# Finishing each target tile of graph attention inside its edge loop, with the turned tiles in the dead rows of the queries

## What is computed

```python
hn = _batch_norm(h, bn1_g, bn1_b)
Q, K, V = (hn @ Wq), (hn @ Wk), (hn @ Wv)          # by heads of 16
score = clip(sum(K[src] * Q[dst]) / 4, -5, 5)
a = exp(score - smax[dst]); a = a / segment_sum(a, dst)[dst]
wV = segment_sum(V[src] * a, dst)
h2 = h + wV @ Wo + bo
h3 = _batch_norm(h2, bn2_g, bn2_b)                 # statistics over all nodes
return h2 + relu(h3 @ W1 + b1) @ W2 + b2
...
aggregated = segment_sum(x[src], tgt)              # the last layer
out = relu((x + aggregated / counts) @ W.T + b)
```

## Time and profile before

| | before |
|---|---|
| median of 3 runs | 1333.84 us (1333.36 to 1334.45) |
| the profiled execution's own time | 1335.18 us |
| its span | 1333.2 us |
| instructions | 18242 |
| PE busy | 990.6 us (74%) |
| DVE busy | 867.2 us (65%) |
| ACT busy | 523.6 us (39%) |
| POOL busy | 413.0 us (31%) |
| mean granted clock of PE | 0.833 |

### The profile page before, as it was taken

How to read it: one execution, slowest core, us unless ns; L and a number is a source line. 1 busy time by engine, 2 the same in 40 slices (tenths; PEclk the granted TensorE clock), 3 DMA queues, 4 the chain that set the end, 5 groups by cost and what they waited for, 6 DMA issues and landing times. The chain is left out here.

```text
span 1333.2 us, 18242 instructions
## 1 busy us (share of the span) xinstructions
PE 990.6 (74%) x6074; PEld 622.3 (47%) x6074; DVE 867.2 (65%) x2126; ACT 523.6 (39%) x1007; POOL 413.0 (31%) x516
## 2 busy tenths in 40 slices
PE   1289989999999998894655565656656565557997
PEld 1168845645556454454433343434434333345554
DVE  4879946734434467466377877777877777764343
ACT  1289913111111111112456555556655556424210
POOL 4000000000000000001277777777777777720000
PEclk9999999999999999896865766666666766568999
DMA  6000061000000000000543333333333333319000
GB/s 156 26 1 1 1 211 34 1 9 0 9 1 0 17 16 23 12 1 24 154 123 104 106 106 104 106 105 106 107 105 106 107 105 105 107 44 226 12 24 26
DMA packets 49496, 87.78 MB, mean 66 GB/s; under 512 B 12384, under 2 KB 35315, under 8 KB 49161
## 3 DMA queue, kind: packets, MB, share of 16 engines
q0 software_dynamic: 20608, 55.20, 14.4%
q1 hardware_dynamic: 26312, 29.89, 8.3%
q10 hardware_dynamic: 2492, 1.61, 0.5%
HBM read 70.68 MB, written 15.98 MB: 65 GB/s over the span
## 5 line engine op out<-in xcount | busy, mean ns | idle before, releaser
L1413 POOL DMA_INDIRECT counts_all<-kv_d,counts_all x416 | 394.4, 948 | 154.7 <-issue 145.9
L867 PE MATMUL bank<-counts_all,parts 125*128 (+2 forms) x1750 | 344.4, 355 | 19.5 <-DVE parts L1047 9.7
L867 PEld LDWEIGHTS bank<-counts_all,parts 125*128 125x128 f16 x1750 | 159.8, 98 | 190.9 <-DVE parts L1047 11.0
L1553 PE MATMUL bank<-counts_all 125*128 125x128 f16 x1230 | 133.9, 288 | 83.3 <-ACT counts_all L1619 82.9
L1299 POOL IOTA iota_n<- 128x256 f16 x1 | 0.3, 349 | 562.1 <-POOLq L854 562.1
L1553 PEld LDWEIGHTS bank<-counts_all 125*128 125x128 f16 x1230 | 110.1, 133 | 126.6 <-ACT counts_all L1619 126.3
L1542 PE MATMUL bank<-rel_rows,ident_h 104*128 104x512 f16 x104 | 56.9, 547 | 124.6 <-ACT away L1609 123.9
L1483 DVE TENSOR_TENSOR counts_all<-counts_all,bank 128x512 f32<-128x512 f32 x104 | 71.5, 687 | 117.6 <-DMA counts_all<-kv_d,counts_all 117.6
L1568 PE MATMUL bank<-counts_all,parts 128*128 128x272 f16 x615 | 135.2, 378 | 14.3 <-DVE counts_all L1461 12.1
L670 PE MATMUL bank<-parts 128*125 128x125 f16 x625 | 102.7, 324 | 12.0 <-DVE parts L589 12.0
L1609 ACT ACTIVATE away<-bank,lane_bias 125x512 f16<-125x512 f32 x173 | 110.8, 680 | 1.0 <-PE bank L1542 0.7
(11 more groups left out here) (268 smaller groups left out, 1264.2 us busy)
## 6 DMA issues: line engine op xcount, KB each, us to landing
counts_d<-counts_all SPq DMA_DIRECT2D x1, 6835.9 KB
counts_all<-counts_d SPq DMA_DIRECT2D x1, 6835.9 KB
counts_all<-kv_d,counts_all POOLq DMA_INDIRECT x416
kv_d<-counts_all SPq DMA_DIRECT2D x6, 448.0 KB
q_d<-counts_all SPq DMA_DIRECT2D x1, 1562.5 KB
x<-in_x SPq DMA_DIRECT2D x6, 250.0 KB
out<-parts SPq DMA_DIRECT2D x6, 250.0 KB
inv_deg<-in_x SPq DMA_DIRECT2D x1, 1400.0 KB
```

What stands on the lines that cost most here:

```text
L867: last = T.matmul(agg_ps[p][:, 0:w], pin[:, s, part, :], counts[:, s, bass.ds(b * BLK, w)], start=(s + part == 0), stop=(s + part == NT))
L1413: G.indirect_dma_start(out=out_rows, out_offset=None, in_=table_d, in_offset=bass.IndirectOffsetOnAxis(ap=index, axis=0)).then_inc(signal, 16)
L1553: last = T.matmul(pick_ps[n % DEEP][:, k * C:(k + 1) * C], ohT[n % DEEP][:, tile - GTILES[n][0], k, :], Q[:, tile, part, :], start=(tile = ...
```

## The change

Division, turning, projection with the residual, and statistics move into the loop. Tile t is divided by DVE right after it is taken (group `LAST_OF[t]` + 3), turned by PE at + 5, projected at + 6, its statistics are taken at + 7. ACT copies what PE made, behind its exponential of the same group. Tiles 0 to 22 are so finished in the loop; tiles 23 and 24 (`LATE`) behind its last sums, one after the other. Turned and projected tiles pass through the two halves of `ps[0]`, the bank of `spread`; so in these groups PE waits until ACT has read the distances, runs the turning or the projection, then the sums, then waits for ACT's copy, and only then spreads. `Q` moves to the end of the arena, and `h2T` is laid over it: tile t over the rows of Q of tile t. Because of that `h2T` lives until the last feed-forward block, and tiles 22 to 24 of the counts return one by one behind `ff_done`, the first seven at once behind the bias steps. The loads of `w1` and `w2` move into SP's queue of the attention block. The last layer's held sums now go up to tile 23 before its stages, and each held stage keeps one tile.

The cores of the diff (the general branch, declarations and the deleted code of the second block are left out):

```diff
+        ARENA_END = NT * N - NT * 2 * C - (NT * N) % 16
+        turned_area = counts_all[:, ARENA_END:ARENA_END + NT * 2 * C]
+        Q = turned_area[0:TILE, :].rearrange("p (t h c) -> p t h c", h=2, c=C)
+        h2T = turned_area.bitcast(fp32).rearrange("p (t c) -> p t c", c=C)[:, :, 0:TILE]
...
+            TURN_AT = {LAST_OF[t] + 5: t for t in range(NT) if LAST_OF[t] + 6 < NG}
+            PROJECT_AT = {LAST_OF[t] + 6: t for t in range(NT) if LAST_OF[t] + 6 < NG}
+            STATS_AT = {LAST_OF[t] + 7: t for t in range(NT) if LAST_OF[t] + 7 < NG}
+            LATE = [t for t in range(NT) if LAST_OF[t] + 6 >= NG]
+            turn_ps, project_ps = ps[0][:, 0:TILE], ps[0][:, LANES:LANES + TILE]
...
+                    sp.dma_start(w1[:, :], W1).then_inc(ff_in, 16)
+                    sp.dma_start(w2[:, :, :], W2.rearrange("(j f) c -> f j c", j=2)).then_inc(ff_in, 16)
                     sp.wait_ge(cols_in, 16 * 7)
                     sp.wait_ge(q_out_done, 16)
...
+                    def divide(tile):
+                        rden_st.run(V.tensor_scalar(rden, acc[:, tile, C:VW], 1e-20, att_scale[0:TILE, V_SCALE:V_SCALE + 1],
+                                                    ALU.max, ALU.mult))
+                        rden_st.run(V.reciprocal(rden, rden))
+                        wv = acc[:, tile, 0:C].rearrange("p (h c) -> p h c", h=HEADS)
+                        V.tensor_tensor(wv, wv, rden.unsqueeze(2).to_broadcast([TILE, HEADS, HD]), ALU.mult).then_inc(wv_ready, 1)
+
+                    def statistics(tile):
+                        dve.wait_ge(h2_copied, tile + 1)
+                        V.bn_stats(bst2[:, tile, :], h2T[:, tile, :]).then_inc(h2_stats, 1)
...
+                    dve.wait_ge(cols_in, 16 * 7)
+                    V.tensor_tensor(bcol6[:, 7:8], bcol6[:, 7:8], bcol6[:, 10:11], ALU.add).then_inc(b2_added, 1)
                     with dve.If(wide <= 1):
...
                             if g >= 3:
                                 take_tiles(g - 3)
+                            if g in STATS_AT:
+                                statistics(STATS_AT[g])
...
+                    pe.wait_ge(cols_in, 16 * 7)
                     with pe.If(wide <= 1):
...
-                            if g + DEEP + 1 < NG:
-                                spread(g + DEEP + 1)
-                            if g >= 2:
+                            ahead = g + DEEP + 1
+                            if g in TURN_AT or g in PROJECT_AT:
+                                pe.wait_ge(away_ready, min(ahead, NG))
+                                if g in TURN_AT:
+                                    turn(TURN_AT[g])
+                                else:
+                                    project(PROJECT_AT[g])
                                 sums(g - 2)
+                                if ahead < NG:
+                                    if g in TURN_AT:
+                                        pe.wait_ge(wvt_copied, TURN_AT[g] + 1)
+                                    else:
+                                        pe.wait_ge(h2_copied, PROJECT_AT[g] + 1)
+                                    spread(ahead)
...
                         sums(NG - 2)
                         sums(NG - 1)
+                        for tile in LATE:
+                            turn(tile)
+                            project(tile)
...
+                    act.wait_ge(b2_added, 1)
+                    act.wait_ge(q_out_done, 16)
                     with act.If(wide <= 1):
...
                             S.activation(VA[g % 2][:, :, C:VW], by_head, ACT.Exp).then_inc(a_ready, 1)
+                            if g in TURN_AT:
+                                copy_turned(TURN_AT[g])
+                            if g in PROJECT_AT:
+                                copy_projected(PROJECT_AT[g])
...
                     sp.wait_ge(bias_step, BIAS_STEPS)
-                    for rows in SPRAY:
-                        sp.dma_start(counts_all[rows, SPILL * N:NT * N], counts_d[rows, :]).then_inc(counts_back, 16)
+                    bring_back(SPILL, NT - 3)
+                    for k in range(3):
+                        tile_end = (NT - 2 + k) * N
+                        held = -(-(tile_end - ARENA_END) // (2 * C))
+                        sp.wait_ge(ff_done, min(-(-held * TILE // BLK), NBLK + 1))
+                        sp.wait_ge(counts_back, 32 * (k + 1))
+                        bring_back(NT - 3 + k, NT - 2 + k)
...
                     pe.wait_ge(u_ready, NBLK + 1)
+                    held_sums(every[NBLK - 1][3], BLK // TILE)
+                    pe.wait_ge(counts_back, 32 * 4)
                     pe.wait_ge(x2_new, NBLK + 1)
```

More of the change, by code:

```diff
@@ L1506, in _ @@
                             take_tiles(n)
+                        for tile in range(len(STATS_AT), NT):
+                            statistics(tile)
                     with dve.Else():
+                        rden_st.n = 0
                         dve.sem_inc(oh_ready, 1)
@@ L1532, in _ @@
                                                 ps[4][0:TILE, 0:VW].unsqueeze(1), ALU.add).then_inc(gen_added, 1)
+                        dve.wait_ge(gen_added, CH * NT + 1)
+                        for tile in range(NT):
+                            divide(tile)
+                        for tile in range(NT):
+                            statistics(tile)
                 @block.tensor
@@ L1570, in sums, with turn, project @@
                         last.then_inc(seg_done, 1)
+                    def turn(tile):
+                        pe.wait_ge(wv_ready, tile + 1)
+                        if tile:
+                            pe.wait_ge(h2_copied, tile)
+                        T.transpose(turn_ps, acc[:, tile, 0:C], ident[0:TILE, 0:TILE]).then_inc(wvt_done, 1)
+                    def project(tile):
+                        pe.wait_ge(wvt_copied, tile + 1)
+                        T.matmul(project_ps, wo[:, :], wvT, start=True, stop=False)
+                        for part in range(2):
+                            last = T.matmul(project_ps, x2[:, tile, part, :], ident_a[0:TILE, 4, :], start=False, stop=(part == 1))
+                        last.then_inc(h2_done, 1)
+                    pe.wait_ge(cols_in, 16 * 7)
                     with pe.If(wide <= 1):
@@ L1626, in high_part, with copy_turned, copy_projected @@
                         S.copy(VAp[n % DEEP][:, 0, :, :], VA[n % 2][:, :, :]).then_inc(hi_part, 1)
+                    def copy_turned(tile):
+                        act.wait_ge(wvt_done, tile + 1)
+                        S.copy(wvT, turn_ps).then_inc(wvt_copied, 1)
+                    def copy_projected(tile):
+                        act.wait_ge(h2_done, tile + 1)
+                        S.activation(h2T[:, tile, :], project_ps, ACT.Identity, bias=bcol6[:, 7:8]).then_inc(h2_copied, 1)
+                    act.wait_ge(b2_added, 1)
+                    act.wait_ge(q_out_done, 16)
                     with act.If(wide <= 1):
@@ L1647, in _ @@
                         high_part(NG - 1)
+                        for tile in LATE:
+                            copy_turned(tile)
+                            copy_projected(tile)
                     with act.Else():
@@ L1797, in stage @@
                         if n < HELD:
-                            for s in range(every[NBLK - 1][3], NT):
-                                last = held_product(s, n)
+                            last = held_product(NT - 1, n)
                         else:
```

117 lines of the change are left out of this document (41 added, 76 removed).

## The result

The changed kernel takes **1346.4 us** (median of 4 runs, 1345.87 to 1347.94); the kernel before, run beside it, 1334.05 us (4 runs, 1333.36 to 1334.45). The ratio is 1.0095, 95% interval 1.0083 to 1.0107. The forecast was 1335.5 us, no difference that can be measured, with 1331.0 to 1341.0 around it: the time lies above the range.

A forecast was written before the change was run, and what follows sets the result against it. POOL's gathers were taken to pace the loop (5.0 us a group), PE what follows. 14.5 - 12.9 + 0.1 = +1.7 took the profiled 1335.18 to 1336.9; less 1.34 for the median, 1335.5 us; 8-in-10 range 1331.0 to 1341.0.

The forecast's parts named there:

- Start of the loop, +14.5: Waits for column loads and Q's store at the loop's start make POOL begin group 3 late: +14.5 us (13.7 to 15.5).
- Rival A: Start of the loop: the column loads land before PE is ready, only the gain counts, about 1321 us; chance 0.12.
- The rule that it weighs: Column loads: a transfer takes a nearly fixed 2.0 us plus its bytes, so columns in near 660, time about 1321.
- Inside the loop: nothing: Attention loop: work added to DVE, PE and ACT per tile costs nothing, since POOL paces the groups.
- the 4.6 us of slack: Attention loop: DVE's weighted values of group G-2 end 4.6 us before POOL's group G+1 needs them.
- Rival B: Attention loop: DVE's added instructions stretch POOL's gathers, 0.45 us once per tile, 10.3 in all, so 1345.8 us; chance 0.13.
- Behind the loop, -12.9: From last sums to first feed-forward product: only two late tiles stay, so that product comes 12.9 us sooner (11.7 to 13.5).
- Rival C: End of the chain: late last weights stall PE 2 to 3 us, or a slow branch jump the same: 1337.5 to 1338.5; chance 0.08.
- Tail, +0.1: Feed-forward to the end: shorter held stages on PE cost one 0.1 us stall, 1.3 at most unless the weights are late.
- Clock, no difference: PE's clock behind the loop: low at the loop's end in both kernels, feed-forward starts low again, no difference counted.

The follow-up runs named there:

- the kernel before with a sum more: Kernel before, with DVE also adding up 2 x 250 constants out of PSUM into PSUM in each group that takes a tile: 1334.33 us (ratio 1.0006).

## Why the prediction was wrong

- **Start of the loop, +14.5: right.** 15.1 by the trace, 15.3 by taking it away. The chain from the column to POOL's group 3 ran as worked out, each link within 0.5 us once the 1.3 us by which the block began earlier are added back. (685.6 less 670.90 is 14.7 and not 14.75, which changes nothing.) Rival A was rightly kept small: the columns came behind the store as in before. The rule that it weighs is given, in the section that it names, for transfers that GpSimd issues; these are SP's.
- **"Inside the loop: nothing": the step that failed.** Its first half holds: from group 3 on POOL idled 122.75 us between its gathers, in before 122.76, so the 4.6 us of slack covered DVE's lateness. It even had the lateness: "A group with a tile had 0.42 us left and gets 0.66 too long". What failed is the inference that lateness within the slack is free. POOL and DVE meet not only at a semaphore but in SBUF, and at one moment: a gather that starts while the low part runs is held until 0.82 us behind its end. In before the low part of a usual group ended just about where a gather starts (49 of 104 already reached over one by less than 0.15 us, none with harm). A delay of DVE by some tenths of a us puts it onto the next start: +10.6, 32 gathers held for 0.36 us on average where in before it was 4.
- **Rival B named the symptom and the size, the size in part by luck, and not the cause.** "Once per tile 10.3, so 1345.8" is near what was measured, but made of 23 gathers at 0.45 us and not of 32 at 0.36; it held the new scalar steps to be the suspects and had 0.13. They are innocent (34 starts under a scalar step by 0.15 us or more, none stretched); the instruction that holds POOL stood in the loop all along. Its argument against, that "DVE's copies and casts per group" leave the median alone, misread the trace: in the loop DVE casts nothing and copies once per taken tile (L1469); the casts are ACT's. The four stretched gathers of before, of which I saw only the maximum of 1394 ns in the earlier trace rows, each lie under a low part: looking up what DVE did at those four would have pointed at it.
- **Behind the loop, -12.9: right in kind, 1.4 too large.** The barrier was taken at 0.33 us and takes 1.97 (1214.38 to 1216.35), because of PE's way past the longer branch (1.7 us by one run, 1.4 by another); the other links were together 0.3 shorter than forecast. Rival C had this jump in half a sentence, at "the same" 2 to 3 us.
- **Tail, +0.1: right** (-0.1); the late weights never stopped PE. **Clock, no difference: right here** (third four passes 11.70 us after the first, 12.00 in before), though in the versions above this stretch lies between 9.62 and 12.95 us.
- **Sum:** 15.1 + 10.6 - 11.5 - 0.1 - 1.3 = +12.8, by the rounded spans 12.7. The last, an earlier start of the loop, belongs to no part of the change: over the traces, also of the kernel before with a sum more, the first gather starts between 653.2 and 655.7.

On the mechanism the Trainium skill, SBUF — State Buffer, section Who interferes with whom, states that a DVE instruction with two inputs in SBUF contends with a GpSimd instruction that reads SBUF, and one with at most one such input, outside DVE's 2-port modes, does not. The runs agree for the low part: 32 of 32 starts held against 0 of 31 with one operand in PSUM. They don't show what the gather needs of SBUF at its start. The same section reports a tensor-tensor form as not having stalled such transfers; here one did, and the measurement decides. I had used its sentence on copies and scalar forms; none of them stretched a gather here.

## What to carry to other kernels

Slack at a semaphore says nothing of collisions: before calling work on an off-path engine free, look where the moved instructions land against the pacing engine's instruction starts, and look up each outlier of the pacing group in the trace of before, for it can name the partner. A wait belongs in front of its first user, not at the head of a block; here that alone was 15 us of a 1334 us kernel. And when a change nets to about nothing, take its terms apart: a gain of 11 us lay under two losses, of which one could be removed wholly and the other for the most part.

## What the hardware showed that I had not expected

- A gather of POOL (0.945 us) that starts under the low part (both operands in SBUF, 0.71 us) 0.15 us or more before its end ends 0.82 us after that end, so it loses the overlap less some 0.13 us: up to 0.54 us. Where the low part begins after the gather has, nothing is lost (23 gathers that began up to 0.3 us ahead of one took at most 0.95 us); so only the start is exposed. With one operand in PSUM the same instruction, 0.71 us long, costs the gather nothing.
- Which of the two waits is decided within hundredths of a us: of gathers that began 0.02 us behind the low part's start neither of two was held, and the low part itself took some 0.06 us longer; from 0.05 us on all 129 were held.
- That every DVE instruction with both operands in SBUF holds a gather is not shown. The only other one that the loop has for each tile, the division's product (0.29 us), lay over a start by 0.15 us or more five times in all versions, each time begun 0.04 us or less ahead of the gather: no gather was held, and the product took 0.32 to 0.36 us.
- The price has an edge: DVE later by some 0.03 us behind each tile (0.05 in the take shown) cost nothing measurable (1.0006), by some 0.3 us (0.37 in the take shown) 0.49%.
- A longer general branch that is never entered costs 1.4 to 1.7 us, once, where PE has to pass it with everyone waiting behind (2.73 us against 1.34 and 1.06); at the start of the block, where the chain had 2.35 us to spare, it did not show.
